# Graph attention block on one core: node table stage rearranged over the queues and tiles, and the exponentials of the edge loop kept in PSUM

## What is computed

```python
xn = _layernorm(x)
# graph attention, 4 heads of 64
h = einsum('nd,hdf->nhf', xn, W)
e = leaky_relu((h*att_src).sum(-1)[src] + (h*att_dst).sum(-1)[dst], 0.2)
ex = exp(e - segment_max(e, dst)[dst])
alpha = ex / segment_sum(ex, dst)[dst]
out = segment_sum(h[src] * alpha[:, :, None], dst).reshape(N, 256) + bias
# x + out + linear attention of xn (RMS norm, q/k/v, w_out, RMS norm)
# then a layer norm and a top-2 of 8 experts, added to x
```

## Time and profile before

| | |
|---|---|
| median of 3 runs | 2803.91 us |
| profiled execution, its span | 2807.02 us, 2805.3 us |
| TensorE, VectorE, ScalarE, GpSimd busy | 56%, 56%, 26%, 68% of the span |
| granted TensorE clock, mean | 0.669 |
| L938, the gathers of the edge loop, GpSimd | 1612 times, 1613.0 us busy, 481.7 us idle ahead of them with nothing waited for |
| L1406, the weighing, VectorE | 403 times, 280.6 us busy |
| bytes moved | 418.73 MB, 149 GB/s over the span |

### The profile page before, as it was taken

One profiled execution on the slowest core, in us unless ns is written; L12 is line 12 of the kernel. 1 busy time (PEld: TensorE's weight loads), 2 busy tenths in 40 slices (PEclk: granted clock), 3 DMA queues, 4 the chain that ended last, 5 costly groups with the idle time before them and its releaser, 6 DMA issues. The chain is left out here.

```text
span 2805.3 us, 54614 instructions
## 1 busy us (share of the span) xinstructions
PE 1582.2 (56%) x17401; PEld 1226.4 (44%) x17401; DVE 1575.3 (56%) x5615; ACT 720.2 (26%) x2125; POOL 1900.6 (68%) x1849
## 2 busy tenths in 40 slices
PE   3656665656666445335426654754575566314995
PEld 2444444545444333224315543543454455213884
DVE  5576676767777565455655645564566556331331
ACT  3622221112222121112104322432343333111221
POOL 1276667777777777777777777777777767644442
PEclk9867766555566555555556876876687677656997
DMA  5245555744454644534464565556556555366887
GB/s 169 88 132 149 151 147 162 207 109 142 135 165 132 158 122 109 147 113 109 119 176 131 161 164 153 143 151 160 170 149 184 158 145 157 83 135 176 218 211 182
DMA packets 275874, 418.73 MB, mean 149 GB/s; under 512 B 70992, under 2 KB 206036, under 8 KB 275336
## 3 DMA queue, kind: packets, MB, share of 16 engines
q0 software_dynamic: 98592, 245.59, 34.1%
q1 hardware_dynamic: 173360, 167.20, 19.6%
q10 hardware_dynamic: 3640, 2.50, 0.3%
HBM read 341.18 MB, written 73.83 MB: 148 GB/s over the span
## 5 line engine op out<-in xcount | busy, mean ns | idle before, releaser
L938 POOL DMA_INDIRECT region<-node_table,region x1612 | 1613.0, 1001 | 644.4 <-issue 481.7
L1165 PE MATMUL ps_p<-region 128*32 128x65 f32 x12896 | 388.8, 287 | 686.3 <-DVE region L1406 683.4
L1165 PEld LDWEIGHTS ps_p<-region 128*32 128x32 f32 x12896 | 299.8, 150 | 784.2 <-DVE region L1406 775.8
L1036 ACT ACTIVATE region<-region 128x16 f32<-128x16 f32 x403 | 87.1, 216 | 1283.7 <-DVE region L1400 1266.8
L1406 DVE TENSOR_TENSOR region<-region 128x512 f32<-128x512 f32 x403 | 280.6, 696 | 132.4 <-DVE region L1390 80.2
L1147 PE MATMUL ps_s<-ident,region 128*128 128x128 f32 x403 | 163.2, 405 | 299.3 <-DVE region L1400 292.4
L1386 DVE TENSOR_SCALAR region<-drep,region 128x8 f32 x403 | 105.2, 261 | 257.7 <-issue 256.8
L1147 PEld LDWEIGHTS ps_s<-ident,region 128*128 128x128 f32 x403 | 94.6, 235 | 323.3 <-DVE region L1400 315.5
L1414 DVE SCALAR_TENSOR_TENSOR acc<-ps_p,region,acc 128x65 f32 x806 | 193.1, 281 | 76.2 <-issue 58.7
L1151 PEld LDWEIGHTS ps_s<-region 128*128 128x128 f32 x806 | 198.3, 275 | 62.9 <-issue 37.1
L1398 DVE TENSOR_TENSOR region<-region,ps_s 128x16 f32<-128x16 f32 x403 | 67.5, 168 | 264.3 <-DMA region<-node_table,region 206.5
(11 more groups left out here) (320 smaller groups left out, 2748.5 us busy)
## 6 DMA issues: line engine op xcount, KB each, us to landing
region<-in_W_dram SPq DMA_DIRECT2D x84, 512.0 KB, 4.7
region<-node_table,region POOLq DMA_INDIRECT x1612
acc<-in_W_dram SPq DMA_DIRECT2D x28, 512.0 KB
acc<-base_rows SPq DMA_DIRECT2D x14, 896.0 KB, 6.1
qkv_rows<-region SPq DMA_DIRECT2D x49, 194.0 KB
region<-expert_in SPq DMA_DIRECT2D x28, 258.0 KB
xe<-expert_in SPq DMA_DIRECT2D x28, 258.0 KB, 4.1
node_table<-region SPq DMA_DIRECT2D x49, 132.0 KB, 1.7
```

The lines of the kernel that those rows point to most:

```text
L938: pool.indirect_dma_start(out=rows[:, s, j, :], out_offset=None, in_=table[:, :], in_offset=bass.IndirectOffsetOnAxis(ap=idx[:, s * SUB + ...
L1165: m = pe.matmul(ps_p[s % 2][h * WIN:(h + 1) * WIN, 0:HC], wts[:, s % 2, j, h, :], rows[:, s, j, h * HC:(h + 1) * HC], start=j == 0, stop=j ...
```

## The change

Part one rearranges the node table stage. ACT's queue keeps the four loads that the graph weight needs, and `loads` counts only those; the other eight go to GpSimd's queue, with a semaphore of their own, `mix_loads`, for which GpSimd waits ahead of its first gather and VectorE ahead of the edge loop. The fill of the row buffer with ones goes from GpSimd to VectorE. Ahead of the tiles VectorE takes only the first group's statistics, not two groups'; the second and the third group's are taken between the first seven tiles (2, 2, 2, 1, 2, 1 and 4 of them). The twelve small operations of a group are spread: `moments` over tiles 0 to 2 in three pairs, `unit_scales` over tiles 4 and 5 in two threes, and ScalarE's roots go ahead of tile 5. Four operations on the edge blocks' columns (`columns_of_blocks`, L1293 to L1296 before) move from the front to behind tile 13. TensorE waits for `weights` at its first product, not at its first transpose.

Part two is in the edge loop: ScalarE writes the exponentials into PSUM, in columns 128 to 143 of the bank that the block's products use, and `weigh` reads them there.

```diff
-def join_moments(dve, own, st, mv, tmp):
+def join_means(dve, own, st, mv, tmp):
     own.do(dve.tensor_tensor(mv[:, :, 0], st[:, :, 1], st[:, :, 4], ALU.add))
     own.do(dve.tensor_scalar(mv[:, :, 0], mv[:, :, 0], 0.5, None, ALU.mult))
+def join_differences(dve, own, st, mv, tmp):
     own.do(dve.tensor_tensor(tmp[:, :], st[:, :, 1], st[:, :, 4], ALU.subtract))
     own.do(dve.scalar_tensor_tensor(out=tmp[:, :], in0=tmp[:, :], scalar=0.25, in1=tmp[:, :], op0=ALU.mult, op1=ALU.mult))
+def join_variances(dve, own, st, mv, tmp):
     own.do(dve.tensor_tensor(mv[:, :, 1], st[:, :, 2], st[:, :, 5], ALU.add))
     own.do(dve.scalar_tensor_tensor(out=mv[:, :, 1], in0=mv[:, :, 1], scalar=1.0 / DIM, in1=tmp[:, :],
                                     op0=ALU.mult, op1=ALU.add))
...
-        N_LOADS = 12
+        N_LOADS, MIX_LOADS = 4, 8
...
+        def ex_ps(s):
+
+            return ps_p[s % 2][:, P:P + SUB * G_HEADS].rearrange("p (j h) -> p j h", h=G_HEADS)
...
-            pool.memset(hrow.rearrange("p s j c -> p (s j) c")[:, :, 0:G_HEADS * HC], 1.0).then_inc(consts, 1)
...
+            pool.dma_start(w_q[:, :, :], g["w_qkv"].rearrange("(c p) n -> p c n", p=P)).then_inc(mix_loads, 16)
+            pool.dma_start(gpre[:, :], g["g_pre"].rearrange("(c p) -> p c", p=P), allow_slow_non_contiguous=True).then_inc(mix_loads, 16)
+            pool.dma_start(bias_row[:, :], g["g_bias"].partition_broadcast(P)).then_inc(mix_loads, 16)
...
+            pool.wait_ge(mix_loads, 16 * MIX_LOADS)
             pool.wait_ge(sd_ready, X_GROUPS)
...
-            act.dma_start(w_q[:, :, :], g["w_qkv"].rearrange("(c p) n -> p c n", p=P)).then_inc(loads, 16)
-            act.dma_start(gpre[:, :], g["g_pre"].rearrange("(c p) -> p c", p=P), allow_slow_non_contiguous=True).then_inc(loads, 16)
-            act.dma_start(bias_row[:, :], g["g_bias"].partition_broadcast(P)).then_inc(loads, 16)
...
-            act.wait_ge(consts, 2)
             for n in range(TILES + 2):
                 if n < TILES:
+                    if n % XG == XG - 2 and n // XG + 1 < X_GROUPS:
+                        deviation(n // XG + 1)
                     if n % XG == 0:
-                        if n // XG + 1 < X_GROUPS:
-                            deviation(n // XG + 1)
                         act.wait_ge(scales, n // XG + 1)
                     if n >= XR:
                         act.wait_ge(xT_ps, n - XR + 1)
                     unit_rows(n, xr_ready)
...
-                act.activation(ex[:, s % 2], lg[:, s % 2], ACT.Exp).then_inc(ex_ready, 1)
+                act.activation(ex_ps(s), lg[:, s % 2], ACT.Exp).then_inc(ex_ready, 1)
...
-            pe.wait_ge(consts, 4)
-            pe.wait_ge(weights, 1)
+            pe.wait_ge(consts, 3)
...
+                if n == 0:
+                    pe.wait_ge(weights, 1)
...
+            dve.memset(hrow.rearrange("p s j c -> p (s j) c")[:, :, 0:G_HEADS * HC], 1.0)
...
+                if part == 0:
+                    own.wait()
+                    join_means(dve, own, st[:, r, :], mv[:, r, :], rstd[:, r])
+                elif part == 1:
+                    join_differences(dve, own, st[:, r, :], mv[:, r, :], rstd[:, r])
+                else:
+                    join_variances(dve, own, st[:, r, :], mv[:, r, :], rstd[:, r])
+                    dve.sem_inc(stats, 1)
...
-            moments(0)
-
-            dve.wait_ge(bases_in, 16)
-            own.do(dve.tensor_scalar(column[0:1, 0:BLOCKS], bases[0:1, :], 5, None, ALU.arith_shift_right))
-            own.do(dve.tensor_scalar(offset[0:1, :], bases[0:1, :], WIN - 1, None, ALU.bitwise_and))
-            own.step(dve.tensor_copy(bases_f[0:1, 0, :], bases[0:1, :]))
-            own.do(dve.tensor_copy(bases_f[0:1, 1, :], offset[0:1, :]))
-            dve.sem_inc(bases_f_ready, 1)
-            unit_scales(0)
-            for n in range(XG, 2 * XG):
-                tile_stats(n)
-            moments(1)
-
+            for k in range(3):
+                moments(0, k)
             dve.wait_ge(loads, 16 * N_LOADS)
-            for i in range(2):
-                for c in range(KC):
-                    own.do(dve.tensor_tensor(tmp, w_h[:, c, 0:DIM], att[:, i, :], ALU.mult))
-                    own.do(dve.tensor_reduce(w_h[:, c, DIM + 4 * i:DIM + 4 * i + 4],
-                                             tmp.rearrange("p (h f) -> p h f", f=F_HEAD), AX.X, ALU.add))
+            logit_weights(0)
+            for k in range(2):
+                unit_scales(0, k)
+            logit_weights(1)
             dve.sem_inc(weights, 1)
 
...
+            FIRST_STATS = (2, 4, 6, 7, 9, 10, 14)
             for n in range(TILES):
                 i, j = n // XG, n % XG
-                if j == 2 and i + 1 < X_GROUPS:
-                    unit_scales(i + 1)
                 rows_back(n)
                 if j == 3 and i:
                     node_logit(i - 1)
-                if i + 2 < X_GROUPS:
+                if i == 0:
+                    for k in range(FIRST_STATS[j - 1] if j else 0, FIRST_STATS[j]):
+                        tile_stats(XG + k)
+                    if j == 3:
+                        for k in range(3):
+                            moments(1, k)
+                elif i + 1 < X_GROUPS and j < 3:
+                    moments(i + 1, j)
+                if i and i + 2 < X_GROUPS:
                     tile_stats(n + 2 * XG)
-                    if j == XG - 1:
-                        moments(i + 2)
+                if i + 1 < X_GROUPS and j in (4, 5):
+                    unit_scales(i + 1, j - 4)
+                if n == XG + 6:
+                    columns_of_blocks()
             node_logit(X_GROUPS - 1)
 
...
-                dve.tensor_tensor(wts[:, s % 2], bcast(mask[:, s], 2, G_HEADS), bcast(ex[:, s % 2], 3, WIN), ALU.mult).then_inc(w_ready, 1)
+                dve.tensor_tensor(wts[:, s % 2], bcast(mask[:, s], 2, G_HEADS), bcast(ex_ps(s), 3, WIN), ALU.mult).then_inc(w_ready, 1)
...
+            dve.wait_ge(mix_loads, 16 * MIX_LOADS)
```

67 lines of the change are left out of this document (41 added, 26 removed).

## The result

The changed kernel takes 2758.31 us (median of four runs, 2752.45 to 2761.22), the kernel before beside it 2805.15 us (2803.89 to 2806.42): a ratio of 0.9825, 95% interval 0.9809 to 0.9841. The forecast was 2748 us, the range 2734 to 2774 us. So the time lies in the range and 10 us above the forecast. The profiled execution took 2761.22 us with a span of 2759.5 us, where before it was 2807.02 and 2805.3 us.

What follows compares the result with a forecast made beforehand. GpSimd's gathers were taken as the loop's clock, starting when the table is done. 29 us from the table stage and 27 us from the loop off 2807.0 us gave 2751 us, median 2748 us; range 2734 to 2774 us.

Steps and rivals of the forecast that it cites:

- Up to the first product: Front of the table stage: the fold waits for four loads, first product at 17.7 us, 22.0 us earlier.
- VectorE's fill locking GpSimd out: Front: if VectorE's new fill blocks GpSimd's, the first moments end at 13.6 us again instead of 10.6.
- Group 0: Table stage, first seven tiles: VectorE is the limit, 10.1 us against 10.7, 0.6 us gained.
- The stalls: TensorE's 2.17 us stops at group boundaries in the table stage: four left go away, 8.7 us.
- crowding: Table stage: VectorE's work just fits a tile, so 0.3 us a boundary is charged, 1.8 us in all.
- Rival (1): Table stage keeps its stalls or the fills block each other: stage gains 15, whole 2762 us; chance 0.13.
- The eight loads on GpSimd: Before the first gather: some 17 us of issue, over before 35 us, costed at nothing.
- The holds: Edge loop: gathers starting inside the weighing lose their 34.9 us of holds with one input in PSUM.
- Rival (2): Edge loop: holds don't depend on the weighing's inputs, or move to another operation; only 29 us come, 2775 us; chance 0.14.
- How much reaches the end: Edge loop: all 23.6 us of holds behind 700 us plus 4 us from earlier arrive, 27 us in sum.
- The prediction's own sign of being wrong: Edge loop: GpSimd's waits for TensorE grow by what its gathers lose; or first gather waits for `mix_loads`.
- The sum: Whole kernel: 2807.0 - 29 - 27 = 2751 us for a profiled-like execution, 3.1 us above the median, so 2748 us.

Runs made afterwards that it cites:

- e3: Changed kernel with all twelve loads on ScalarE's queue and the fold waiting for twelve: 3188.31 us on a chip where the kernel before takes 3189.33 us.
- e9: Kernel before with only the exponentials moved into PSUM: 2792.24 us, 0.9946 of the kernel before (2807.85 us).
- e11: Changed kernel with exponentials back in SBUF and each block's second accumulation on VectorE left out: 2759.23 us, 0.9834 of the kernel before.
- e12: Changed kernel, exponentials in PSUM, with each block's second accumulation on VectorE left out: 2744.91 us, 0.9774 of the kernel before.
- e1_table_only: Changed kernel with the exponentials back in SBUF, only the table stage changed: 3135.22 us, 0.9918 of the kernel before (3162.06 us).

## Why the prediction held, and where it didn't

**Up to the first product: right.** Forecast 17.7 us, measured 18.51 us; the gain is 21.2 us for 22.0. The fold began at 12.87 us for 12.2, when the last of the four loads had landed; the moments ended at 10.5 us, as the scaling took 0.32 us for 3.31 (it starts 0.15 us before GpSimd's fill ends). The bound on which a loss hung, VectorE's fill locking GpSimd out, did not come true: that fill took 3.09 us from 1.68 us (some 4 us were forecast; at the rate of L1406, which the forecast names, it would be 4.9 us) and left GpSimd's 6.60 us as they were. e3 confirms the step by undoing it.

**Group 0: right.** 9.8 us for a forecast of 10.1. **The stalls: right, with a charge that wasn't due.** From tile 7 to the last the stage got 9.65 us shorter. The forecast was 8.7 less 1.8 us for crowding, 6.9 us. The wait at tile 7 is 0.36 us; the only one over 0.5 us behind it is 0.69 us at 39.9 us, where VectorE has the four column operations. With 0.2 us behind the last tile the 31.9 us are complete: 21.2 + 0.9 + 9.65 + 0.2. Rival (1), which ends at 2762 us, came nearer to the time than the forecast did, and yet none of it happened.

**The eight loads on GpSimd: right, mis-sized.** They were issued from 10.25 to 16.3 us, 6 us in all for an estimate of 17; a load costs 0.5 to 1.1 us, also the two with 512 pieces of 4 bytes, for which the gather's price would be 3.8 us. Nobody waited for them.

**The holds: right in kind.** They went, all of them, with the one input in PSUM. Rival (2) is refuted. The operations changed too, which the forecast had put at nothing: the exponential got 28 ns shorter (216 to 188) and the weighing 9 ns, 37 ns in a chain that runs 403 times. That product, 14.9 us, is as long as the loop's gain, but it doesn't explain it: in gathers 640 to 1280 the loop's time follows the gathers' busy time within 1.2 us. How much the shorter chain brings in the rest is not shown. The forecast of the gathers' busy time, 1578 us, is what e9 shows; the changed kernel has 1585.3 us. Of these 7.0 us more 5.0 us lie in gathers of less than 1.0 us: an unheld gather mostly takes 957 ns in this trace and 953 ns in those of before and e9, for a reason that stayed open. The other 2.1 us are gathers of 1.0 us and more, which other operations hold.

**How much reaches the end: wrong.** This is the step that failed: the holds behind 700 us were taken to arrive whole, 23.6 us, and with what lies ahead of them 27 us; 14.3 us arrived. I split the loop at gather 320 (570 us). All sums are of what a gather takes over 0.953 us, and of waits beyond the usual 0.31 us:

| | first 320 gathers | the rest |
|---|---|---|
| time in weighing holds, less | 9.7 us | 24.1 us |
| all other gather time, more | 0.8 us | 5.4 us |
| waits, more | 7.6 us | 5.7 us |
| loop time saved | 1.4 us | 12.9 us |
| forecast | some 3 us | 24 us |

In the first part the forecast was about right in kind: a gather that is done sooner waits longer for its slot. GpSimd's timelines show it at one place of the loop, at its 80th and 81st gathers, before and after. The 80th is held before and no longer after, and the 81st waits 1.18 us where it waited 0.74:

```profile
224.65 1.15 POOL L938 DMA_INDIRECT region<-node_table,region  x1 [0.30 <-issue]
226.54 0.95 POOL L938 DMA_INDIRECT region<-node_table,region  x1 [0.74 <-issue]
```

```profile
192.16 0.96 POOL L966 DMA_INDIRECT region<-node_table,region  x1 [0.30 <-issue]
194.29 0.96 POOL L966 DMA_INDIRECT region<-node_table,region  x1 [1.18 <-PE ps_p L1184]
```

In the rest half arrives. 5.4 us go to other gather time, some of it the 957 ns above, and 5.7 us to waits. The waits grew where there were few before: by 1.8 us in gathers 320 to 480 (from none), by 1.7 us in 480 to 640 and by 2.1 us in 1280 to 1440; in 640 to 1280 they did not grow, and there the gathers' 7.5 us brought 7.2 us. The reading that GpSimd is the clock in 1000:1300 was right for that stretch and on to about 1955 us, and was carried over to all that lies behind 700 us. The prediction's own sign of being wrong, that GpSimd's waits for TensorE grow by what its gathers lose, came true for 12.5 of 27.7 us. e11 and e12 show that VectorE's load alone does not decide how much arrives where GpSimd has waits; TensorE's and ScalarE's part was not tried on a chip where it would show.

**The sum.** 29 + 27 us were forecast, 31.9 + 14.3 us came. That the time lies in the range is due to the width of the range, and in small part to luck: the stage's 2.9 us more offset some of the loop's 12.7 us less. The offset between the profiled execution and the median, for which 3.1 us stood, was 2.9 us.

## What to carry to other kernels

A saving on the busiest engine is worth what remains after its waits have grown again. So look for the waits it already has in every stretch, not only in the one where it is fullest: here the saving arrived whole where it had none, for a small part where it had some, and not at all on a chip where it had many. A long VectorE operation with two SBUF inputs beside GpSimd's gathers holds a gather almost to the end of that one instruction: put an input in PSUM, or cut the operation. Ahead of a first dependent step, wait for the loads that it reads and for no others.

## What the runs showed that was not expected

- The same kernel takes 2805 to 2808 us on some chips and 3162 to 3189 us on others, with the same granted clock, 0.50, in 1000:1300 of the loop. There TensorE pauses inside its rows of products, 92.6 us of 300 in e1_table_only. A change that brings 0.5% on one chip measures 1.0006 on the other.
- A gather that meets a cut operation waits for the current piece alone, although the next piece follows at once: 1.05 us in place of 1.65 us in the example, and 0.1 to 0.25 us of mean hold for the pieces of the row updates in place of 0.8 to 1.2 us for the whole operations.
- Two fills of SBUF, VectorE's of 3640 values and GpSimd's of 7800, ran beside each other for 1.9 us without lengthening GpSimd's, 6.60 us both before and after.
